# Graph attention kernel: the one-hot comparisons of a pair in two wide 16-bit instructions, and the first transform outside the pair loop

## The reference

```python
def rgat_conv(x, W, q, k, b, src, dst, etype, heads, out_ch, n_nodes):
    xr = jnp.einsum('nd,rdf->rnf', x, W)
    oi = xr[etype, dst]
    oj = xr[etype, src]
    alpha = jax.nn.leaky_relu(oi @ q + oj @ k, NEG_SLOPE)
    m = jax.ops.segment_max(alpha, dst, num_segments=n_nodes)
    e = jnp.exp(alpha - m[dst])
    z = jax.ops.segment_sum(e, dst, num_segments=n_nodes)
    a = e / (z[dst] + EPS)
    msg = (a[:, :, None] * oj.reshape(-1, heads, out_ch)).reshape(-1, heads * out_ch)
    return jax.ops.segment_sum(msg, dst, num_segments=n_nodes) + b
...
h = jax.nn.elu(rgat_conv(x, W1, q1, k1, b1, src, dst, edge_type, HEADS1, OUT1, n))
out = rgat_conv(h, W2, q2, k2, b2, src, dst, edge_type, HEADS2, OUT2, n)
x = _layernorm(x + out, axis=-1)
```

## Time and profile before

| | us |
|---|---|
| median of 3 runs | 1508.04 (1505.2 to 1508.9) |
| profiled execution, its own time | 1509.87 |
| its span | 1508.1 |
| PE busy | 1325.4 (88%) |
| DVE busy | 1142.0 (76%) |
| ACT busy | 731.6 (49%) |
| POOL busy | 6.5 |
| mean granted TensorE clock, share of full speed | 0.934 |

### The profile page before, as it was taken

The page is one execution under the profiler, slowest core; times in us unless marked ns, Lnnn a source line. Parts: engine busy times, 40 slices in busy tenths (PEclk is TensorE's granted clock), DMA queues, the critical chain, the costliest instruction groups (busy, mean ns, idle before and its releaser), DMA issues.

```text
span 1508.1 us, 20272 instructions
## 1 busy us (share of the span) xinstructions
PE 1325.4 (88%) x7162; PEld 1190.1 (79%) x7162; DVE 1142.0 (76%) x1875; ACT 731.6 (49%) x1243; POOL 6.5 (0%) x19
## 2 busy tenths in 40 slices
PE   1899999999834999999999999897579899975995
PEld 1898555556523999999999999897569899974995
DVE  2776999996895998998989976756536577744875
ACT  1542331110105997997989952245424345633462
POOL 1000000000000000000000000000000000000000
PEclk9886999999956999999999999999789999997998
DMA  5440013111104333342333226743257756654561
GB/s 192 180 147 0 35 40 105 53 53 42 53 0 140 98 94 94 98 129 90 97 94 90 59 95 220 262 140 122 98 208 281 229 202 199 201 192 137 181 215 50
DMA packets 84904, 189.01 MB, mean 125 GB/s; under 512 B 7479, under 2 KB 59182, under 8 KB 84818
## 3 DMA queue, kind: packets, MB, share of 16 engines
q1 hardware_dynamic: 84626, 187.39, 37.5%
q0 software_dynamic: 192, 0.45, 0.1%
HBM read 148.21 MB, written 41.53 MB: 126 GB/s over the span
## 4 chain that ended last, share of the span: by engine, by line
PE 69%; DVE 14%; DMA 9%; ACT 4%; issue 3%; SPq 0%; DVEq 0%; ACTq 0%; POOL 0%; POOLq 0%
PE ps L1020 20%; PE ps L1075 19%; PE ps L872 14%; PE ps L901 5%; PE ps L918 4%; DVE arena L1208 3%; DVE arena L1351 3%; PE ps L857 2%; DMA x2a<-xr_d 2%; PE ps L848 1%; DMA arena<-in_L_gnn_W 1%; DVE arena L1268 1%; DVE arena L1272 1%; DMA arena<-in_x 1%; DMA out<-arena 1%
## 5 line engine op out<-in xcount | busy, mean ns | idle before, releaser
L1020 PE MATMUL ps<-arena 128*128 128x193 f32 x2400 | 398.1, 328 | 1.8 <-DVE arena L1272 1.5
L1020 PEld LDWEIGHTS ps<-arena 128*128 128x128 f32 x2400 | 393.6, 190 | 4.2 <-DVE arena L1272 3.6
L872 PE MATMUL ps<-arena,xT 128*128 128x384 f32 x720 | 243.8, 489 | 0.0
L655 ACT ACTIVATE arena<-arena,misc 128x640 f32<-128x640 f32 x240 | 197.0, 821 | 42.4 <-DVE arena L1268 23.6
L872 PEld LDWEIGHTS ps<-arena,xT 128*128 128x128 f32 x720 | 132.7, 191 | 80.1 <-issue 0.6
L656 ACT ACTIVATE arena<-arena,misc 128x640 f32<-128x640 f32 x240 | 195.6, 815 | 0.0
L1268 DVE TENSOR_TENSOR arena<-arena 128x1280 f32<-128x1280 f32 x120 | 178.4, 1487 | 20.1 <-ACT arena L656 17.7
L1272 DVE SCALAR_TENSOR_TENSOR arena<-arena,Ct 128x1280 f32<-128x1280 f32 x120 | 179.1, 1492 | 14.5 <-DVE arena L1268 10.1
L1075 PE MATMUL ps<-g_hi,x2b 128*128 128x418 f32 (+1 forms) x540 | 153.9, 354 | 27.5 <-DVE g_lo L1425 27.5
L1075 PE MATMUL ps<-g_hi,x2a 128*128 128x418 f32 (+1 forms) x540 | 156.3, 359 | 18.2 <-DVE g_lo L1425 10.6
L1208 DVE SCALAR_TENSOR_TENSOR arena<-arena,misc 128x1250 f32<-128x1250 bf16 x108 | 156.7, 1515 | 0.0
(11 more groups left out here) (173 smaller groups left out, 1613.1 us busy)
## 6 DMA issues: line engine op xcount, KB each, us to landing
x2a<-xr_d SPq DMA_DIRECT2D x41, 768.0 KB, 4.7
x2b<-xr_d SPq DMA_DIRECT2D x41, 768.0 KB, 4.4
arena<-xr_d SPq DMA_DIRECT2D x120, 193.0 KB, 2.4
xr_d<-stg SPq DMA_DIRECT2D x60, 384.0 KB, 3.0
arena<-ab_d SPq DMA_DIRECT2D x12, 1280.0 KB, 6.4
arena<-in_L_gnn_W SPq DMA_DIRECT2D x6, 2304.0 KB, 9.1
xr_d<-arena SPq DMA_DIRECT2D x30, 386.0 KB, 2.8
arena<-in_L_gnn_W SPq DMA_DIRECT2D x6, 1152.0 KB, 6.6
```

Of the source, the lines that this page charges most:

```text
L655: nc.scalar.activation(e1[t % 5][:, h, :], abr[:, r, h, :], ACT.Exp, bias=qk1t[:, t, col + R * H:col + R * H + 1])
L872: last = mm(ps[2 + 2 * (t % 2) + b][:, 0:HF], xT[:, kt, t * P:(t + 1) * P], weights(WOFF[1] + r)[:, kt, b * HF:(b + 1) * HF], start=kt == ...
L1020: last = mm(bank1(g, i)[:, o:o + HD + 1], e1[t % 5][:, h, i * P:(i + 1) * P], xring[t % NX][:, o:o + HD + 1], start=False, stop=True, skip ...
```

## The change

VectorE's codes are copied once into 16-bit buffers `slo_b` and `mcode_b` in which the six runs of a pair are adjacent. The constant ramps are made wide by GpSimd, each value six times (`i_sp`, 128 x 6, and `i_mp`, 240 x 6). The one-hot matrices of a pair are stored with the run index innermost, and each of the two is built by one TENSOR_TENSOR, of 768 and of 1440 elements. The count matmuls read run n of them, so both their operands have a step of six 16-bit elements.

In the pair loop TensorE's other work is spread out: the 18 transpose sets come in pairs 1, 3, 6, 8, 11, ... 43 (WT_AT), the products two pairs later (WQ_AT), the logits in pairs 48, 51, ... 75 (LG_AT). No transform is left in the loop; all three stand behind it. The transposes for reductions 0 now stand in the second transform from its tile 5 on, those for reductions 1 in the third transform from its tile 1 on (MK_AT = (5, 1)). In maxima 2 the reductions of type 1 come five behind tile 8 and five behind tile 9 (RED1_AT = 8), in place of two behind each tile from 5 on.

```diff
-        slo_w = edi.bitcast(F32).rearrange("p (w t) -> p w t", t=RUN)
...
+        slo_b, mcode_b = (edi.bitcast(F32)[:, i * NE // 2:(i + 1) * NE // 2].bitcast(BF16) for i in range(2))
+        PT = 2 * RUN
+        ohs_p = [take(PT * P // 2).bitcast(BF16).rearrange("p (s n) -> p s n", n=PT) for _ in range(2)]
+        ohm_p = [take(PT * WM // 2).bitcast(BF16).rearrange("p (m n) -> p m n", n=PT) for _ in range(2)]
...
+            nc.gpsimd.iota(i_sp, [[1, P], [0, PT]], base=0, channel_multiplier=0, **io).then_inc(S["wide_in"], 1)
+            nc.gpsimd.iota(i_mp, [[1, WM], [0, PT]], base=0, channel_multiplier=0, **io).then_inc(S["wide_in"], 1)
...
-        LOGITS_AT = R * KT + 2
-        T_AT = LOGITS_AT + NT
-        RED1_AT = 5
-        MK_AT = 5
+        WT_AT = {1 + 5 * i // 2: i for i in range(R * KT)}
+        WQ_AT = {p + 2: i for p, i in WT_AT.items()}
+        LG_AT = {max(WQ_AT) + 3 + 3 * t: t for t in range(NT)}
+        RED1_AT = 8
+        MK_AT = (5, 1)
...
-                        n = (h * 2 + c) * RUN + t
-                        last = mm(ps[h][:, c * WM:(c + 1) * WM], ohs[n], ohm[n], start=t == 0, stop=t == RUN - 1)
+                        n = c * RUN + t
+                        last = mm(ps[h][:, c * WM:(c + 1) * WM], ohs_p[h][:, :, n], ohm_p[h][:, :, n], start=t == 0, stop=t == RUN - 1)
                 last.then_inc(S["c_done"], 1)
...
+            for r in range(R):
+                for t in range(NT):
+                    for kt in range(KT):
+                        if r:
+                            n = (t - MK_AT[r - 1]) * KT + kt
+                            if 0 <= n < NT:
+                                mk_transpose(r - 1, n)
+                        transform_tile(r, t, kt)
+
             mk_transposes(2)
             ab_transposes(L1)
...
-            link(V.tensor_copy(slo_w.rearrange("p (s w) t -> p s t w", s=2), slo.rearrange("p (s t w) -> p s t w", s=2, t=RUN)))
+            for o, v in ((slo_b, slo), (mcode_b, mcode)):
+                link(V.tensor_copy(o.rearrange("p (s w t) -> p s t w", s=2, t=RUN), v.rearrange("p (s t w) -> p s t w", s=2, t=RUN)))
...
+            dve.wait_ge(S["wide_in"], 2)
             with dve.Fori(0, 2) as s:
                 with dve.Fori(0, SW // 4) as j:
                     for h in range(2):
                         dve.wait_ge(S["c_done"], s * (SW // 2) + j * 2 + (h + 1))
 
-                        w = slo_w[:, bass.ds(s * SW + j * 4 + h * 2, 2), :]
-                        V.tensor_tensor(oh_s[:, h * 2 * RUN:(h + 1) * 2 * RUN, :].rearrange("p (c t) s -> p c t s", c=2),
-                                        i_s[:, :].unsqueeze(1).unsqueeze(1).broadcast_to([P, 2, RUN, P]),
-                                        w.unsqueeze(3).broadcast_to([P, 2, RUN, P]), ALU.is_equal)
-                        for c in range(2):
-                            for t in range(RUN):
-                                col = s * (RUN * SW) + j * 4 + (t * SW + h * 2 + c)
-                                last = V.tensor_scalar(ohm[(h * 2 + c) * RUN + t], i_m[:, :], mcode[:, bass.ds(col, 1)], None, ALU.is_equal)
-                        last.then_inc(S["oh"], 1)
+                        col = s * (RUN * SW) + j * (4 * RUN) + h * PT
+                        V.tensor_tensor(ohs_p[h], i_sp, slo_b[:, bass.ds(col, PT)].unsqueeze(1).broadcast_to([P, P, PT]), ALU.is_equal)
+                        V.tensor_tensor(ohm_p[h], i_mp, mcode_b[:, bass.ds(col, PT)].unsqueeze(1).broadcast_to([P, WM, PT]), ALU.is_equal).then_inc(S["oh"], 1)
...
                     if r == R - 1 and t >= RED1_AT:
-                        for s in range(2):
-                            reduce1(1, 2 * (t - RED1_AT) + s)
+                        for s in range(NT // 2):
+                            reduce1(1, NT // 2 * (t - RED1_AT) + s)
```

More of the change, by code:

```diff
@@ L162, in rgat @@
         mcode = take(NE)
-        slo_w = edi.bitcast(F32).rearrange("p (w t) -> p w t", t=RUN)
[L164 to L167, removed]
+        slo_b, mcode_b = (edi.bitcast(F32)[:, i * NE // 2:(i + 1) * NE // 2].bitcast(BF16) for i in range(2))
+        PT = 2 * RUN
+        ohs_p = [take(PT * P // 2).bitcast(BF16).rearrange("p (s n) -> p s n", n=PT) for _ in range(2)]
+        ohm_p = [take(PT * WM // 2).bitcast(BF16).rearrange("p (m n) -> p m n", n=PT) for _ in range(2)]
+        ohs = [ohs_p[0].rearrange("p s n -> p (s n)")[:, i * P:(i + 1) * P] for i in range(4)]
+        ohm = [ohm_p[0].rearrange("p m n -> p (m n)")[:, i * WM:(i + 1) * WM] for i in range(4)]
+        i_sp = take(PT * P // 2).bitcast(BF16).rearrange("p (s n) -> p s n", n=PT)
+        i_mp = take(PT * WM // 2).bitcast(BF16).rearrange("p (m n) -> p m n", n=PT)
+        assert pos[0] <= 2 * WS + 2 * H * NP
         x_sb = Ct[:, :, :].rearrange("p a b -> p (a b)")[:, 0:2 * NT * F].bitcast(F32).rearrange("p (t f) -> p t f", t=NT)
@@ L315, in rgat @@
         PAIRS = NW // 2
-        LOGITS_AT = R * KT + 2
-        T_AT = LOGITS_AT + NT
-        RED1_AT = 5
-        MK_AT = 5
+        WT_AT = {1 + 5 * i // 2: i for i in range(R * KT)}
+        WQ_AT = {p + 2: i for p, i in WT_AT.items()}
+        LG_AT = {max(WQ_AT) + 3 + 3 * t: t for t in range(NT)}
+        assert max(LG_AT) < PAIRS - 1
+        RED1_AT = 8
+        MK_AT = (5, 1)
         HT_AT = [0, 3, 6]
@@ L608, in _ @@
                 last.then_inc(S["c_ready"], 1)
[L609 to L614, removed]
+                if pair - 1 in WT_AT:
+                    wt_out(L1, WT_AT[pair - 1])
+                if pair - 1 in WQ_AT:
+                    wq_out(L1, WQ_AT[pair - 1])
+                if pair - 1 == max(LG_AT):
                     logits(L1)
-                if k >= T_AT and (k - T_AT) % KT == KT - 1:
-                    transform_out((k - T_AT) // KT)
             def ab_rows(lay):
@@ L624, in ab_rows @@
                 last.then_inc(S["ab_rows"], 1)
-            for n in range((PAIRS - 1 - T_AT) // KT, RS):
+            for n in range(RS):
                 transform_out(n)
@@ L875, in transform_tile @@
                     last.then_inc(S["t_done"], 1)
[L877 to L880, removed]
             def unit(u):
@@ L916, in _ @@
                     for t in range(RUN):
-                        n = (h * 2 + c) * RUN + t
-                        last = mm(ps[h][:, c * WM:(c + 1) * WM], ohs[n], ohm[n], start=t == 0, stop=t == RUN - 1)
+                        n = c * RUN + t
+                        last = mm(ps[h][:, c * WM:(c + 1) * WM], ohs_p[h][:, :, n], ohm_p[h][:, :, n], start=t == 0, stop=t == RUN - 1)
                 last.then_inc(S["c_done"], 1)
[L920 to L927, removed]
+                if pair in WT_AT:
+                    wt_transposes(L1, WT_AT[pair])
+                if pair in WQ_AT:
+                    wq_product(L1, WQ_AT[pair])
+                if pair in LG_AT:
+                    logits(L1, LG_AT[pair])
             pe.wait_ge(S["flag_ready"], 1)
```

2 lines of the change are left out of this document (1 added, 1 removed).

## The result

The changed kernel is slower: 1618.9 us against 1507.0, a ratio of 1.0745 with an interval of 1.0706 to 1.0784. I had predicted 1489 us with a range up to 1524: wrong in sign, and 95 us above the range; no case of the prediction, the dearest at 1568 us, reached it. The profiled execution took 1617.4 us, its span 1615.6, at a granted clock of 0.887 over the whole run (0.934 before).

What follows compares the result with a forecast made beforehand. VectorE was taken to bound the late pairs of the count loop, TensorE the early ones. Loop 71.4 us shorter, stretch behind it 52.1 longer: -19.3 us, 1490.6 in the profiled execution, 1489 us as median; range 1476 to 1524.

Steps and rivals of the forecast that it cites:

- A reads slower: Rival, count matmuls: TensorE's reads at 12-byte steps cost up to 1.22 us per pair, 1504 to 1523 us; chance 0.25.
- the term of the loop: Count loop: 45 pairs at 1.48 us, 34 at 1.29, logits 2 us; its end at 165 us instead of 236.4.
- the cycle of five pairs, followed: Pairs 1 to 45: TensorE has 6.9 us, VectorE 6.45; with 0.5 us of waiting, 7.4 us per five pairs.
- the main forecast: Whole kernel: 1489 us, its own range 1478 to 1498, chance 0.45.
- the clock falls late: Rival, loop from pair 46 on: half clock makes 72 us of 46.7, loop end 190, 1514 us; chance 0.13.
- The build: One-hots of each pair: two TENSOR_TENSOR at doubled pace, 0.55 and 0.90 us, 1.29 us per pair.
- VectorE stays at one element a time: Rival, every build: 2.45 us per pair, 1568 us; chance 0.09 together with a loop at half clock throughout.
- VectorE sets the pace of the late pairs: Last 34 pairs of the count loop: VectorE's builds set 1.29 us each, 43.9 us.
- Behind the loop: Transforms, maxima and reductions: TensorE waits 17 and 2.5 us, last reduction 273.2 us behind the loop, stretch 52.1 us longer.
- the kernel without the first wait: Rival, third transform: TensorE's 17 us wait does not come, 1469 us; chance 0.06.
- The new iotas and the second copy: Before the loop: iotas of 0.8 and 1.5 us and a 0.50 us copy, hidden; at most 3 us otherwise.
- the expected gain: Count loop: TensorE leaves it 71.4 us earlier, at 165 us instead of 236.4.

Runs made afterwards that it cites:

- experiment 4: Changed kernel with count operands read from a constant ramp, moving operand at steps 1 to 9, then weights at 1 to 16, counts wrong; one execution, 1563.2 us.
- experiment 1: Changed kernel with both operands of the count matmuls read as adjacent elements, counts wrong; 1516.5 us, ratio 1.008 to the kernel before.
- experiment 5: Changed kernel with one-hots stored in three groups of two, so TensorE reads at a step of 2 elements; 1518.3 us, ratio 1.0059 to the kernel before.
- experiment 2: Changed kernel with only the moving operand of the count matmuls read as adjacent elements, counts wrong; 1523.0 us, ratio 1.0103 to the kernel before.
- Experiment 6: Changed kernel with type 1 reductions two behind each tile of the third maxima from tile 5, their transposes two ahead per tile; 1593.3 us, ratio 1.0569.
- experiment 9: Changed kernel with both the groups-of-two one-hots (step 2) and the type 1 reductions spread over the third maxima from tile 5; 1493.3 us, ratio 0.9901.
- 12: Kernel with step 2 builds and 35 transform steps in the loop, ten of these one pair earlier, ahead of products or logits; 1466.2 us, ratio 0.9718.
- 10: Step 2 builds, transposes, products and logits in the pairs of the kernel before, 35 transform steps in the loop, reductions placed anew; 1474.0 us, ratio 0.9764.
- experiments 7: Kernel before, its schedule kept, with the two wide comparisons in groups of two (step 2 builds); 1504.1 us, ratio 0.9975.
- 11: Step 2 builds, old pairs for transposes, products and logits, 25 transform steps in the loop, none in pairs 20 to 29; 1474.1 us, ratio 0.9775.
- experiment 8: Changed kernel's schedule with the builds of the kernel before (one comparison of 768, six of 240, adjacent reads); 1550.1 us, ratio 1.0282.

## Why the prediction was wrong

**The step that failed is the rival "A reads slower", in its upper bound, and with it the term of the loop.** I held the count block at 0.61 us, and let the rival go up to 1.22, from a matmul that streams adjacent 4-byte columns. That row had adjacent reads, so it bounded nothing about reads at a step. The prediction cited the rule on 16-byte lines that spoke against the change and gave the case 0.25, but only up to 1523 us. The measured block is 1.93 us, and experiment 4 shows why: the price is in the span of the read. By the prediction's own sums, the 45 pairs with transposes and products take (5 x 1.93 + 3.84) / 5 = 2.70 us each instead of 1.48, 55 us more, and the 34 pairs behind them 34 x 1.93 + 10 x 1.26 = 78 instead of 46. That makes the loop's end 252 us at full clock. The other 37 us are the clock, as an estimate: transposes, products and logits are 47 us of work at full clock, and the loop ran mostly at half, where each costs nearly double (a block of logits 2.39 us in the chain of waits, 1.26 counted). The prediction priced the two rivals one at a time; here both came together, and their costs add.

**A second step failed: the cycle of five pairs, followed.** With reads that cost nothing (experiment 1) the loop still ended 23 us late and the time was 1516.5, so the main forecast would have been missed too. Some 10 us of it come with the wait for ScalarE's copy, a term that the prediction put at nothing without a reason; most of the rest is the lower clock, from the loop's start on and in part, not from pair 46 on. That 1514, the time of the rival "the clock falls late", lies near is luck.

**The build: right.** 0.56 and 0.90 us. The rival that VectorE stays at one element a time is refuted, in the changed kernel and with runs of two in experiment 5.

**VectorE sets the pace of the late pairs: wrong.** TensorE does, in every pair. This kernel's builds went from 2.02 to 1.29 us and the count blocks that read them from 0.61 to 1.93. Where the reads are cheap (experiments 1, 2 and 5) TensorE does wait for the builds in the late pairs, about 1 us in every three pairs.

**Behind the loop: right, step by step.** VectorE's maxima start 2.6 us behind the loop's end (2.2 predicted), TensorE waits 17.1 us (17) and 2.4 us (2.5), and the last reduction ends 274.9 us behind the loop (273.2). Experiment 6 puts a price of 25.6 us on these waits, which could have been avoided without touching the rest. The prediction had the kernel without the first wait at 1469 us, 20 us less, as a rival, and did not take it as a fault to mend.

**The new iotas and the second copy: no cost at the loop's start, but the iotas were mis-sized.** They took 2.53 and 4.58 us, where the prediction had 0.8 and 1.5. Up to the end of the second, at 10.38 us, a VectorE instruction on 160 elements took 2.14 us in place of 0.24, and the indirect DMA behind them started at 13.10 in place of 11.44. The next indirect DMA started at 22.77, against 22.70 before, so the delay was gone by then. The first count matmul starts at 47.5 us, 1.3 sooner than predicted; that is no gain of the change, since the first build starts anywhere from 44.8 to 47.4 us in the traces of the other kernels.

**Where the expected gain went.** Of the 71.4 us that the loop was to end earlier, experiment 9 got 44.3 (loop end at 192.1); its stretch behind the loop is longer by 30, with all 180 transform steps behind it. TensorE had room in the loop for part of the work that was moved out: with 35 of the 50 steps back in the loop, and the other work in its old pairs (12), the loop ends only 8.4 us later, and what is behind it is shorter by 38 us.

## What to carry to other kernels

An operand layout is paid by its writer and by its reader. Before a layout is turned round for a faster write, price the reader's step with a run of its own, and let a row bound it only if it reads that way. When two rivals can be true at once, price them together. Between the two ends there is often a middle: runs of two 16-bit elements gave VectorE its doubled pace and cost TensorE next to nothing (0.64 us a block for 0.61). And moving work out of a loop pays only if the other stretch has room: after each gain on one engine, count both engines again on both sides of the loop's end.

## What the runs showed of the hardware

- A moving operand read at a step costs by the 16-byte line: 0.10 to 0.11 us for 240 bf16 columns at steps 1 and 2, 0.22 at 4, 0.32 at 6, about 0.43 at 8 and 9 (experiment 4). The changed kernel's 0.32 us was the same at both levels of the clock. Weights at steps up to 16 elements didn't slow the blocks. They are not quite free: the mean load went from 115 ns in experiment 1 to 140 in experiment 2, where only the weights had the step, and the loop's end was 10.8 us later; part of both can be a lower clock (0.70 from 140 to 200 us, 0.94 from 140 to 188 in experiment 1), which the runs don't tell apart.
- While a GpSimd iota of 1440 16-bit elements ran (4.58 us), a VectorE instruction that started under it did not end before it (2.14 us in the changed kernel, 1.84 in experiment 1, both ending at 10.48, 0.1 us behind the iota). In experiment 5, where the iotas were over by 7.50, it took 0.24. What holds VectorE is not shown.
- The clock fell at 93 to 99 us in all kernels with the old order of transposes and products, with TensorE busy throughout, on the last pairs of the products, whatever came behind. When the transform's 384-column steps followed it was back after 3.4 us (12) or 20 us (10), in the one traced execution of each; with logits alone it took until 138 to 139.5 us (experiments 7 and 11 and the kernel before). In the changed order it stood at 0.83 to 0.84 from 60 to 140 us with TensorE busy 89 to 90% of the time (experiments 1 and 5), and in experiment 8 at 0.91 to 1.00 until 140 us with it busy 76 to 81%. What decides the fall stays open.
